# An expert layer whose tiles run two narrow experts, two wide, two narrow, two wide, instead of four wide and then four narrow

## The chip, the core and the metric

The kernel runs on one core of one Trainium2 chip. The metric is the device time of one execution in microseconds. A core has a matrix engine (TensorE, PE in the rows; its weight loads are PEld), a vector engine (VectorE, DVE), an engine for activations (ScalarE, ACT), GpSimd (POOL) and SyncE (SP), which here only issues transfers and passes on permissions. Each runs its own program, and they meet at semaphores.

## The reference, cut to what matters

A token embedding with a depthwise convolution over 31 positions, an attention layer that is linear in the sequence, and a mixture of experts, each added to the running `h`. 8 sequences of 512 tokens, 256 channels. The change concerns the expert layer:

```
EXPERT_SIZES = [(4, 256), (4, 512)]      # experts 0-3 narrow, 4-7 wide
probs = sigmoid(xf @ router_w.T)         # xf: 4096 tokens x 256
topw, sel = top_k(probs, 2)              # two experts a token
topw = topw / (topw.sum(-1) + 1e-20)
h = square(relu(xf @ W1e))               # 256 -> 256 or 512
y = h @ W2e                              # 256 or 512 -> 256
out = sum over the two chosen experts of weight * y
```

Float32 products are made of three products of parts (high by high, low by high, high by low).

## The kernel before, in words

**Up to 505 us** the kernel convolves, attends, and routes each batch. VectorE computes for each of a token's two choices a row in a queue in memory (`queue_d`), which has one stretch of rows for each expert, and GpSimd writes the token there with an indirect transfer. `expert_no` maps the eight positions of that order to experts: positions 0 to 3 are the wide experts, 4 to 7 the narrow ones. The weights in the core's memory (`w1_first`, `w1_second`, `w2_hi`, `w2_lo`) lie in the order of positions, each with room for 512 columns; GpSimd clears the half that a narrow expert leaves (lines 845 to 853 and 1576 to 1578).

**The table.** After the last batch VectorE turns the counts of the experts into a table, in a chain of tiny operations that each wait for the one before (`chained`, from line 1221): for each tile of 128 queue rows its first row, its expert (`word_of`, eight tiles in a register's value, three bits each) and `apart`, 16 where a tile has another expert than the tile before it and 0 elsewhere.

**The expert stage** takes 71 tiles of 128 rows, which is the most that any routing can need. For this input the counts of tokens that the reference's own router gives are 1122, 690, 757, 1416 for the narrow experts and 1410, 792, 824, 1181 for the wide ones, so in tiles 9, 6, 6, 12 and 12, 7, 7, 10: 69 tiles with tokens and two of filler. In the order before, tiles 0 to 35 are wide, 36 to 68 narrow, and expert changes lie at tiles 12, 19, 26, 36, 45, 51, 57 and 69 (the filler).

Step j of the pipeline does on TensorE `up(j)`, the turning of x for tile j+2, `act_turn(j-1)` and `down(j-2)`; on ScalarE `relu(j)`, `x_hi(j+2)`, `a_hi(j-1)` and `y(j-2)`; on VectorE `act_w(j)` and the low parts. Two steps make a turn; steps 2n and 2n+1 are turn n. `all_turns` (lines 1522 to 1538) asks once a turn, with a branch on each of the three engines, which width the turn has, and every fourth turn each loads the next word of the table (turns 0, 4, 8, ...). Before the change the width of a turn is that of its oldest tile, 2n-2: with the wide tiles first this is never too narrow. A turn is wide or narrow as a whole.

**The adds.** `y` has four places (`RING`). Tile j's y is added into the output by an indirect transfer from GpSimd (line 1583), and `y(j)` on ScalarE waits until the add of tile j-4, which had the same place, has landed. SyncE permits each add (`allow`, line 1553; its `sem_inc` on line 1563): it waits for `y_ready`, and then for the three adds before, in one of two ways. Tiles of one expert hold different tokens, so their adds may be in flight together. At a tile of another expert (`apart` is 16) all adds before it must have landed. And the first adds have constants for waits, where the value in the register cannot be zero:

```
if before < RING:
    sp.wait_ge(added[before % RING], 16)
else:
    wait_apart(sp, added[before % RING], differs16 + 16 * (before // RING), sp_passed)
```

so adds 1, 2, 3 and 4 each wait until the add ahead of them has landed, whatever their experts.

## Time and profile before

| | us |
|---|---|
| median of 3 runs (lowest to highest) | 737.45 (732.85 to 738.35) |
| the profiled execution | 736.28 |
| its span, first to last instruction | 734.6 |
| share of the span in which TensorE is busy | 86% |
| the chain that ended last: share of TensorE | 65% |
| the same: transfer of the adds (out<-y) | 5% |
| the expert stage, first product to the end | 509.79 to 734.6 |

The page gives each engine's busy time and its share of the span, the span in 40 slices, and the chain of work that ended last. In the slices TensorE stands at 9 tenths and more in the wide part of the expert stage, and at 8 in the narrow part. A busy TensorE is not one at its peak, since the ends of its products are modelled. The granted clock is given as a share of 2.4 GHz: 1.00 is that level and 0.50 is 1.2 GHz. Rows of a timeline begin with the start in us and the duration in us; a bracket gives the idle time ahead and what ended it.

### The profile page before, as it was taken

What the parts mean: (1) busy time and instruction counts of PE and PEld (TensorE: products, weight loads), DVE (VectorE), ACT (ScalarE), POOL (GpSimd) and SP (SyncE); (2) the same over time, 40 slices, a digit from 0 to 9 for tenths busy, and PEclk for the clock granted to TensorE, in tenths of its full rate; (3) what the DMA queues carried; (4) which work ended last, traced back from release to release, by engine and by line L of the source; (5) the groups of instructions that cost most, each with busy time, mean ns of one, the idle gap of its engine ahead of it and who ended that gap; (6) DMA issues with size and microseconds to landing.
All of it is one profiled execution on the core that took longest, in us unless ns stands there. A gap on an engine that the chain in (4) does not pass through costs nothing.

```text
span 734.6 us, 15772 instructions
## 1 busy us (share of the span) xinstructions
PE 632.1 (86%) x5032; PEld 547.8 (75%) x5032; DVE 469.7 (64%) x1216; ACT 306.8 (42%) x668; POOL 322.0 (44%) x292
## 2 busy tenths in 40 slices
PE   6997579999999999999999997523999999988881
PEld 6897457787877878778778785512899999987871
DVE  6475585777779777797787963573554554555540
ACT  3460135343353443533435335330544544555541
POOL 6350250330814608237073260635254454466574
PEclk9999689999999999999999999855999999999996
DMA  6551990010111101112010010423355445466663
GB/s 227 191 105 23 207 341 11 2 57 3 58 58 52 66 1 60 57 45 73 2 59 30 31 57 2 143 95 108 52 83 81 75 82 81 76 112 111 106 97 45
DMA packets 37216, 58.12 MB, mean 79 GB/s; under 512 B 5726, under 2 KB 31066, under 8 KB 36506
## 3 DMA queue, kind: packets, MB, share of 16 engines
q1 hardware_dynamic: 22434, 36.14, 16.9%
q0 software_dynamic: 14160, 20.13, 15.3%
q8 instruction: 61, 1.00, 0.6%
q10 hardware_dynamic: 520, 0.51, 0.2%
q14 instruction: 41, 0.34, 0.2%
HBM read 28.30 MB, written 27.42 MB: 76 GB/s over the span
## 4 chain that ended last, share of the span: by engine, by line
PE 65%; DVE 11%; DMA 7%; issue 5%; ACT 5%; POOL 3%; SPq 3%; DVEq 0%; POOLq 0%; ACTq 0%
PE bank L1311 20%; PE bank L1703 16%; PE bank L1383 8%; DMA out<-y,token_at 5%; PE bank L1354 4%; PE bank L1371 2%; PE bank L1719 2%; PE bank L521 2%; PE bank L522 2%; DVE xn L1009 2%; PE bank L542 2%; PE bank L1340 2%; POOL out L1583 2%; ACT k_exps L895 2%; DVE row L1089 1%
## 5 line engine op out<-in xcount | busy, mean ns | idle before, releaser
L1583 POOL DMA_INDIRECT out<-y,token_at x71 | 111.6, 1572 | 109.7 <-SPq L1563 107.6
L839 POOL DMA_INDIRECT queue_d<-row,slot x64 | 68.8, 1075 | 165.8 <-DVE slot L1148 148.7
L1660 DVE SCALAR_TENSOR_TENSOR act_w<-relu,queue_rows 128x512 f32<-128x512 f32 (+1 forms) x71 | 44.6, 629 | 102.5 <-ACT relu L1606 52.3
L1311 PE MATMUL bank<-xt_hi,w_first 128*128 128x512 f32 x256 | 95.1, 417 | 0.9 <-DVE second_half L1026 0.9
L1311 PE MATMUL bank<-w_first,xt_hi 128*128 128x512 f32 x256 | 83.8, 409 | 2.2 <-DVE xt_lo L1016 1.5
L831 POOL TENSOR_TENSOR second_half<-second_half,q_inv 128x512 f32<-128x512 f32 x64 | 64.9, 1041 | 44.0 <-DVE q_inv L1035 43.8
L887 ACT ACTIVATE second_half<-second_half 128x512 f32<-128x512 f32 x64 | 39.6, 632 | 87.9 <-DVE second_half L1026 87.9
L895 ACT ACTIVATE k_exps<-bank,k_negmax 128x512 f32<-128x512 f32 x64 | 44.1, 690 | 75.3 <-DVE k_negmax L1042 75.1
L1703 PE MATMUL bank<-w_hi,a_hi 128*128 x214 | 66.0, 308 | 1.6 <-DVE a_lo L1666 1.1
L1703 PE MATMUL bank<-w_lo,a_hi 128*128 x214 | 59.9, 280 | 0.1
L1606 ACT ACTIVATE relu<-bank 128x512 f32<-128x512 f32 (+1 forms) x71 | 35.4, 498 | 58.7 <-PE bank L1703 57.9
L1703 PE MATMUL bank<-w_hi,a_lo 128*128 x214 | 59.6, 278 | 0.0
L1311 PEld LDWEIGHTS bank<-w_first,xt_hi 128*128 128x128 f32 x256 | 46.9, 192 | 15.6 <-issue 2.7
L1383 PE MATMUL bank<-g,wv_t 128*128 128x256 f32 x256 | 56.7, 380 | 1.2 <-ACT g L877 1.2
L1311 PEld LDWEIGHTS bank<-xt_hi,w_first 128*128 128x128 f32 x256 | 49.2, 192 | 11.3 <-DVE second_half L1026 1.8
L1023 DVE TENSOR_REDUCE q_max<-bank 128x8 f32<-128x512 f32 x64 | 42.1, 657 | 22.6 <-PE bank L1311 22.6
L1383 PEld LDWEIGHTS bank<-g,wv_t 128*128 128x128 f32 x256 | 48.6, 190 | 8.4 <-ACT g L877 1.6
L1042 DVE TENSOR_REDUCE k_negmax<-bank 128x1 f32<-128x512 f32 x64 | 42.8, 680 | 13.4 <-PE bank L1311 13.1
L1311 PE MATMUL bank<-w_first,xt_lo 128*128 128x512 f32 x128 | 50.9, 398 | 0.0
L1311 PE MATMUL bank<-xt_lo,w_first 128*128 128x512 f32 x128 | 50.8, 397 | 0.0
L1703 PE MATMUL bank<-w_first,x_hi 128*128 x142 | 40.1, 364 | 9.7 <-DVE x_lo L1648 6.5
L1693 PE MATMUL bank<-ident,queue_rows 128*128 128x128 f32 x142 | 27.7, 279 | 23.3 <-DMA queue_rows<-queue_d 23.3
(183 smaller groups left out, 1564.3 us busy)
## 6 DMA issues: line engine op xcount, KB each, us to landing
queue_rows<-queue_d SPq DMA_DIRECT2D x71, 129.0 KB, 2.3
store<-in_L_ffn_w SPq DMA_DIRECT2D x4, 1536.0 KB, 9.2
out<-res SPq DMA_DIRECT2D x8, 512.0 KB, 2.9
h_d<-store SPq DMA_DIRECT2D x6, 512.0 KB, 9.0
h_in<-h_d SPq DMA_DIRECT2D x6, 512.0 KB, 4.0
windows<-taps_d SPq DMA_DIRECT2D x4, 512.0 KB, 5.8
wqk<-in_L_attn_w_qkv SPq DMA_DIRECT2D x1, 2048.0 KB, 13.9
out<-y,token_at POOLq DMA_INDIRECT x71, 4.0
```

The costliest lines, as they stand in the source:

```text
L831: nc.gpsimd.tensor_tensor(v, v, q_inv[:, b.par, u].unsqueeze(2).to_broadcast([P, 8, DH]), ALU.mult).then_inc(q_ready, 1)
L839: pool.indirect_dma_start(out=queue_d, in_=row[:, t, c, :], in_offset=None, out_offset=bass.IndirectOffsetOnAxis(ap=slot[:, TT * c + t:TT ...
L887: nc.scalar.activation(v, v, ACT.Exp, scale=SCALE).then_inc(q_exp_ready, 1)
L895: nc.scalar.activation(k_exps[:, c % 2], qk_bank(10 + c)[:], ACT.Exp, bias=k_negmax[:, c:c + 1], accum_out=k_sum[:, b.par, c:c + 1]).then_ ...
L1023: link(nc.vector.tensor_reduce(q_max[:, u % 2], src, AX, ALU.max), q_chain, b, Q_LINKS, 2 * u + 1 - (u > 0))
L1042: nc.vector.tensor_reduce(k_negmax[:, c:c + 1], qk_bank(10 + c)[:], AX, ALU.max, negate=True).then_inc(k_max_ready, 1)
L1311: last = nc.tensor.matmul(o, a, c, start=(n == 1), stop=(n == 3 * len(pairs)))
L1383: last = nc.tensor.matmul(tail_bank(6)[:, DIM * kk:DIM * kk + DIM], wv_t[:, a, P * kk:P * kk + P], g[:, a], start=(a == 0), stop=(a == PAI ...
L1583: pool.indirect_dma_start(out=out, in_=y[:, j % RING, :], in_offset=None, compute_op=ALU.add, out_offset=bass.IndirectOffsetOnAxis(ap=toke ...
L1606: nc.scalar.activation(relu[:, u % 2, 0:width], bank[2 + u % 2][:, 0:width], ACT.Relu).then_inc(relu_ready, 1)
L1660: nc.vector.scalar_tensor_tensor(out=act_w[:, u % 2, 0:width], in0=relu[:, u % 2, 0:width], scalar=rows[:, u, DIM:DIM + 1], in1=relu[:, u ...
L1703: last = nc.tensor.matmul(o, a, c, start=(n == 1), stop=(n == parts))
```

## The change

The order of positions becomes two narrow, two wide, two narrow, two wide: positions 0, 1, 4, 5 are experts 0 to 3 and positions 2, 3, 6, 7 experts 4 to 7. So a position is wide when its second bit is set. The pieces in which the weights are split and the halves that are cleared follow (lines 605 and following, `w1_pads`, the w2 pads). Filler tiles take position 0, a narrow one, where they took 7.

The width of a turn now comes from a new table, `kind_of`, of one bit for a turn: set when any of the four tiles 2n-2 to 2n+1 is wide. VectorE computes it at the end of the table's chain. All three engines load it every eighth turn; only TensorE still loads `word_of`. Since a narrow turn can now come ahead of a wide one, the upper halves of `act_w`, `a_hi` and `a_lo` are read before anything wrote them, and GpSimd clears them once, after the table is ready. ScalarE, VectorE and TensorE wait for that.

With the counts above, tiles 0 to 14 are narrow, 15 to 33 wide, 34 to 51 narrow, 52 to 68 wide and the two of filler narrow. Expert changes lie at tiles 9, 15, 27, 34, 40, 52, 59 and 69. Turns 0 to 6, 18 to 25 and 36 are narrow, and 7 to 17 and 26 to 35 wide: 21 wide turns, where turns 0 to 18 were wide, 19. Adds 1 to 4 wait as before.

```diff
--- before
+++ changed
@@ -79,6 +79,8 @@
 TABLE = -(-TILES // SLOTS) * SLOTS
 FILLERS = TABLE - TOKENS * TOPK // P
 TURN = 2
+TURNS = -(-(TILES + AHEAD) // TURN)
+TURN_WORDS = -(-TURNS // SLOTS)
 RING = 4
 TOTAL_W = sum(WIDTHS)
@@ -127,6 +129,7 @@
         self.tile_no = sbuf("tile_no", [1, TABLE])
         self.row_of = sbuf("row_of", [1, TABLE], I32)
         self.word_of = sbuf("word_of", [1, TABLE // SLOTS], I32)
+        self.kind_of = sbuf("kind_of", [1, TURN_WORDS], I32)
         self.apart = sbuf("apart", [1, TABLE], I32)
         self.consts, self.filler_ready, self.ends_ready, self.filled, self.chain, self.ready = (sem(n) for n in (
@@ -602,16 +605,16 @@
     r = store[:, n % 3]
     if n < KC:
         own = NARROW * NARROW_W
-        return [(r[:, 0:own].rearrange("p (e w) -> p e w", w=NARROW_W),
-                 dst[:, WIDE * MAXW:].rearrange("p (e w) -> p e w", w=MAXW)[:, :, 0:NARROW_W]),
-                (r[:, own:], dst[:, 0:WIDE * MAXW])]
+        dst = dst.rearrange("p (h e w) -> p h e w", h=2, w=MAXW)
+        return [(r[:, 0:own].rearrange("p (h e w) -> p h e w", h=2, w=NARROW_W), dst[:, :, 0:2, 0:NARROW_W]),
+                (r[:, own:].rearrange("p (h e w) -> p h e w", h=2, w=MAXW), dst[:, :, 2:4])]
     r = r.rearrange("p (c n) -> p c n", n=DIM)
     if n == KC:
-        return [(r[:, 0:8].rearrange("p (e c) n -> p e (c n)", c=2),
-                 dst[:, WIDE * FC:].rearrange("p (e c) n -> p e (c n)", c=FC)[:, :, 0:2 * DIM]),
-                (r[:, 8:12], dst[:, 0:4])]
-    return [(r, dst[:, 4:WIDE * FC])]
+        return [(r[:, 0:8].rearrange("p (h e c) n -> p h e (c n)", h=2, c=2),
+                 dst[:].rearrange("p (h e c) n -> p h e (c n)", h=2, c=FC)[:, :, 0:2, 0:2 * DIM]),
+                (r[:, 8:12], dst[:, 2 * FC:3 * FC])]
+    return [(r[:, 0:4], dst[:, 3 * FC:4 * FC]), (r[:, 4:12], dst[:, 6 * FC:8 * FC])]
 def attend(nc, ctx, sem, bank, ident, base, base0, rw_t, w1, w2, h_d, store, h_in, loaded, h_stored, raw_in,
@@ -767,10 +770,10 @@
         nc.gpsimd.memset(minus_half[:], -0.5).then_inc(consts_pool, 1)
         nc.gpsimd.memset(before[:], 1.0).then_inc(consts_pool, 1)
         nc.gpsimd.memset(every[:], 1.0).then_inc(consts_pool, 1)
-        nc.gpsimd.iota(expert_no[:, 0:WIDE], [[1, WIDE]], base=NARROW, channel_multiplier=0,
-                       allow_small_or_imprecise_dtypes=True).then_inc(consts_pool, 1)
-        nc.gpsimd.iota(expert_no[:, WIDE:], [[1, NARROW]], base=0, channel_multiplier=0,
-                       allow_small_or_imprecise_dtypes=True).then_inc(consts_pool, 1)
+        by_kind = expert_no[:].rearrange("p (h k e) -> p k h e", h=2, k=2)
+        for kind in range(2):
+            nc.gpsimd.iota(by_kind[:, kind], [[2, 2], [1, 2]], base=NARROW * kind, channel_multiplier=0,
+                           allow_small_or_imprecise_dtypes=True).then_inc(consts_pool, 1)
         nc.gpsimd.iota(base0[:], [[QROWS, EXPERTS]], base=0, channel_multiplier=0,
                        allow_small_or_imprecise_dtypes=True).then_inc(consts_pool, 1)
         nc.gpsimd.iota(base[:], [[QROWS, EXPERTS]], base=0, channel_multiplier=0,
@@ -848,9 +851,8 @@
             pool.wait_ge(tail_psum, last.nth(TAIL_USES, 2))
             for kk in range(KC):
                 for part in range(2):
-                    pad = w1_parts[kk][:, part].bitcast(F32)[:, WIDE * MAXW:]
-                    nc.gpsimd.memset(pad.rearrange("p (e w) -> p e w", w=MAXW)[:, :, NARROW_W:MAXW], 0.0
-                                     ).then_inc(w1_zero, 1)
+                    pad = w1_parts[kk][:, part].bitcast(F32).rearrange("p (h e w) -> p h e w", h=2, w=MAXW)
+                    nc.gpsimd.memset(pad[:, :, 0:2, NARROW_W:MAXW], 0.0).then_inc(w1_zero, 1)
         def step(b, prev, nxt, old):
             enqueue(old)
@@ -1211,9 +1213,9 @@
         space, at = x2_t[:].rearrange("p k n -> p (k n)"), [0]
-        def taken(rows, n):
+        def taken(rows, n, within=space):
             at[0] += n
-            return space[0:rows, at[0] - n:at[0]]
+            return within[0:rows, at[0] - n:at[0]]
         passed = taken(1, TABLE * EXPERTS).rearrange("p (t e) -> p t e", e=EXPERTS)
         upto_tiles = taken(P, EXPERTS * EXPERTS).rearrange("p (t e) -> p t e", e=EXPERTS)
@@ -1249,7 +1251,31 @@
         chained(nc.vector.memset(differs[:, 0:1], 0.0))
         chained(nc.vector.tensor_tensor(differs[:, 1:], expert_f[:, 1:], expert_f[:, 0:TABLE - 1], ALU.not_equal))
         chained(nc.vector.tensor_scalar(table.apart[:], differs, 16.0, None, ALU.mult))
-        chained(nc.vector.tensor_scalar(expert_f, expert_f, float(EXPERTS - 1), None, ALU.min))
+        chained(nc.vector.tensor_scalar(differs, expert_f, float(EXPERTS) - 0.5, -float(EXPERTS), ALU.is_gt, ALU.mult))
+        chained(nc.vector.tensor_tensor(expert_f, expert_f, differs, ALU.add))
+        done, at[0] = passed.rearrange("p t e -> p (t e)"), 0
+        wide_i, wide = taken(1, TABLE, done).bitcast(I32), taken(1, TABLE, done)
+        in_pair, in_turn = taken(1, TABLE // TURN, done), taken(1, TURN_WORDS * SLOTS, done)
+        turns2, turns4 = (taken(1, TURN_WORDS * SLOTS // m, done) for m in (2, 4))
+        chained(nc.vector.tensor_copy(wide_i, expert_f))
+        chained(nc.vector.tensor_scalar(wide_i, wide_i, 1, 1, ALU.logical_shift_right, ALU.bitwise_and))
+        chained(nc.vector.tensor_copy(wide, wide_i))
+        pairs = wide.rearrange("p (n u) -> p n u", u=TURN)
+        nc.vector.memset(in_turn, 0.0)
+        chained(nc.vector.tensor_tensor(in_pair, pairs[:, :, 0], pairs[:, :, 1], ALU.max))
+        chained(nc.vector.tensor_copy(in_turn[:, 1:TABLE // TURN + 1], in_pair))
+        chained(nc.vector.tensor_tensor(in_turn[:, 0:TABLE // TURN], in_turn[:, 0:TABLE // TURN], in_pair, ALU.max))
+        pairs = in_turn.rearrange("p (n u) -> p n u", u=2)
+        chained(nc.vector.scalar_tensor_tensor(out=turns2, in0=pairs[:, :, 1], scalar=2.0, in1=pairs[:, :, 0],
+                                               op0=ALU.mult, op1=ALU.add))
+        pairs = turns2.rearrange("p (n u) -> p n u", u=2)
+        chained(nc.vector.scalar_tensor_tensor(out=turns4, in0=pairs[:, :, 1], scalar=4.0, in1=pairs[:, :, 0],
+                                               op0=ALU.mult, op1=ALU.add))
+        pairs = turns4.rearrange("p (n u) -> p n u", u=2)
+        chained(nc.vector.scalar_tensor_tensor(out=table.kind_of[:], in0=pairs[:, :, 1], scalar=16.0,
+                                               in1=pairs[:, :, 0], op0=ALU.mult, op1=ALU.add))
         pairs = expert_f.rearrange("p (n u) -> p n u", u=2)
         chained(nc.vector.scalar_tensor_tensor(out=word2, in0=pairs[:, :, 1], scalar=float(EXPERTS),
@@ -1520,17 +1546,20 @@
         if value > 0:
             engine.wait_ge(s, value)
-    def all_turns(engine, step):
-        words = []
-        for first in range(0, TILES + AHEAD, TURN):
-            if first % SLOTS == 0 and first < TILES:
+    def all_turns(engine, step, by_expert=False):
+        words, kinds = [], []
+        for n in range(TURNS):
+            first = n * TURN
+            if n % SLOTS == 0:
+                kinds.append(engine.value_load(table.kind_of[0:1, n // SLOTS:n // SLOTS + 1], min_val=0,
+                                               max_val=2 ** SLOTS - 1))
+            if by_expert and first % SLOTS == 0 and first < TILES:
                 words.append(engine.value_load(table.word_of[0:1, first // SLOTS:first // SLOTS + 1], min_val=0,
                                                max_val=EXPERTS ** SLOTS - 1))
-            oldest = max(first - AHEAD, 0)
-            with engine.If(((words[oldest // SLOTS] >> (3 * (oldest % SLOTS))) & (EXPERTS - 1)) < WIDE):
+            with engine.If(((kinds[-1] >> (n % SLOTS)) & 1) > 0):
                 for j in range(first, first + TURN):
                     step(words, j // SLOTS, j % SLOTS, MAXW)
             with engine.Else():
@@ -1574,10 +1603,12 @@
     def gpsimd(pool):
         attention_left(pool)
         for w in (w2_hi, w2_lo):
-            pad = w[:].bitcast(F32)[:, WIDE * FC:].rearrange("p (e c) n -> p e (c n)", c=FC)
-            nc.gpsimd.memset(pad[:, :, 2 * DIM:], 0.0).then_inc(pads_zero, 1)
+            pad = w[:].bitcast(F32).rearrange("p (h e c) n -> p h e (c n)", h=2, c=FC)
+            nc.gpsimd.memset(pad[:, :, 0:2, 2 * DIM:], 0.0).then_inc(pads_zero, 1)
         pool.wait_ge(table.ready, 1)
+        for beyond in (act_w, a_hi, a_lo):
+            nc.gpsimd.memset(beyond[:].bitcast(F32)[:, :, NARROW_W:], 0.0).then_inc(pads_zero, 1)
         for j in range(TILES):
             pool.wait_ge(may_add, j + 1)
             pool.indirect_dma_start(
@@ -1634,6 +1665,7 @@
         x_high(0, 0)
         x_high(1, 1)
         act.wait_ge(table.ready, 1)
+        act.wait_ge(pads_zero, 5)
         all_turns(act, step)
     def vector(dve):
@@ -1682,6 +1714,7 @@
         x_low(0, 0)
         x_low(1, 1)
         dve.wait_ge(table.ready, 1)
+        dve.wait_ge(pads_zero, 5)
         all_turns(dve, step)
     def tensor(pe):
@@ -1745,7 +1778,7 @@
             if j == 2:
                 pe.wait_ge(w2_lo_ready, 2)
-                pe.wait_ge(pads_zero, 2)
+                pe.wait_ge(pads_zero, 5)
             if 2 <= j <= TILES + 1:
                 down(j - 2, u, expert_at(words, j - 2), width)
@@ -1754,7 +1787,7 @@
         pe.wait_ge(table.ready, 1)
         pe.wait_ge(w1_lo_ready, KC)
         pe.wait_ge(w1_zero, 2 * KC)
-        all_turns(pe, step)
+        all_turns(pe, step, by_expert=True)
     return Programs(sync, gpsimd, scalar, vector, tensor)
```

ScalarE where the expert stage begins (`w_hi` is the high part of the second weights, `x_hi` that of the first two tiles). Before:

```order
L1594 ACTIVATE w_hi<-store 128x1024
L1594 ACTIVATE w_hi<-store 128x3072 [waits raw_in3]
L1601 ACTIVATE x_hi<-bank 128x256 [waits x_turned] x2
L1530 TENSOR_LOAD word_of [waits table_ready]
L1530 ISA x2
L1533 REGISTER_ALU
L1533 COMPARE_AND_BRANCH
L1606 ACTIVATE relu<-bank 128x512 [waits up_done]
```

and with the change:

```order
L1625 ACTIVATE w_hi<-store 128x1024
L1625 ACTIVATE w_hi<-store 128x1024 [waits raw_in3]
L1625 ACTIVATE w_hi<-store 128x2048
L1632 ACTIVATE x_hi<-bank 128x256 [waits x_turned] x2
L1557 TENSOR_LOAD kind_of [waits pads_zero,table_ready]
L1557 ISA x2
L1562 REGISTER_ALU
L1562 COMPARE_AND_BRANCH
L1637 ACTIVATE relu<-bank 128x512 [waits up_done]
```

The last piece of the second weights is two operations instead of one, and the first relu stands behind a wait for GpSimd's clearing.

GpSimd in the same place, from the last writes to the queue on. Before:

```order
L839 DMA queue_d<-row,slot 34816x258 [waits slots_ready]
L839 DMA queue_d<-row,slot 34816x258 x7
L1578 MEMSET w_hi 128x4x512 [waits stored1,stored0]
L1578 MEMSET w_lo 128x4x512
L1583 DMA out<-y,token_at 4224x256 [waits may_add,table_ready]
```

and with the change:

```order
L842 DMA queue_d<-row,slot 34816x258 [waits slots_ready]
L842 DMA queue_d<-row,slot 34816x258 x7
L1607 MEMSET w_hi 128x2x2x512 [waits stored1,stored0]
L1607 MEMSET w_lo 128x2x2x512
L1611 MEMSET act_w 128x2x256 [waits table_ready]
L1611 MEMSET a_hi 128x2x256
L1611 MEMSET a_lo 128x2x256
L1614 DMA out<-y,token_at 4224x256 [waits may_add] x71
```

The three clearings of 512 numbers a partition stand behind the two that were there, and ahead of the adds.

## Rows read from the trace of the kernel before

**Rows 1.** Windows of 10 us, one wide and one narrow: busy times, clock, DMA

```profile
core 0: us, PE busy (x) PEld busy (x) DVE busy (x) ACT busy (x) POOL busy (x), PEclk, DMA share, GB/s
600.00:610.00 10.00, 10.00 (x73) 9.17 (x72) 5.23 (x12) 5.25 (x12) 4.66 (x3) 1.00 0.48 76
660.00:670.00 10.00, 8.84 (x76) 8.46 (x74) 5.45 (x18) 5.83 (x18) 5.36 (x5) 1.00 0.60 99
```

**Rows 2.** Waits from 640 to 735 us: total us, times, longest us

```profile
ACT y L1618 <- DMA out<-y,token_at: 14.4, 12, 2.8
```

**Rows 3.** Timeline of ScalarE: y of tiles 0, 35, 49 and 68

```profile
519.55 0.38 ACT L1618 ACTIVATE y<-bank 128x256 f32<-128x256 f32 x1 [0.89 <-PE bank L1703]
...
640.00 0.38 ACT L1618 ACTIVATE y<-bank 128x256 f32<-128x256 f32 x1 [0.66 <-PE bank L1703]
...
672.94 0.39 ACT L1618 ACTIVATE y<-bank 128x256 f32<-128x256 f32 x1 [2.17 <-DMA out<-y,token_at]
...
717.15 0.39 ACT L1618 ACTIVATE y<-bank 128x256 f32<-128x256 f32 x1 [0.27 <-PE bank L1703]
```

**Rows 4.** Timeline of ScalarE: relu of the first step of turns 22, 23, 24

```profile
654.57 0.38 ACT L1606 ACTIVATE relu<-bank 128x256 f32<-128x256 f32 x1 [0.96 <-PE bank L1703]
...
658.97 0.39 ACT L1606 ACTIVATE relu<-bank 128x256 f32<-128x256 f32 x1 [1.02 <-PE bank L1703]
...
663.83 0.38 ACT L1606 ACTIVATE relu<-bank 128x256 f32<-128x256 f32 x1 [1.51 <-PE bank L1703]
```

**Rows 5.** Timeline of GpSimd: adds 0, 3, 4, 35, 43, 44, 45, 68

```profile
520.75 1.61 POOL L1583 DMA_INDIRECT out<-y,token_at  x1 [13.84 <-SPq L1563]
...
533.48 1.56 POOL L1583 DMA_INDIRECT out<-y,token_at  x1 [2.77 <-SPq L1563]
539.32 1.70 POOL L1583 DMA_INDIRECT out<-y,token_at  x1 [4.27 <-SPq L1563]
...
641.74 1.55 POOL L1583 DMA_INDIRECT out<-y,token_at  x1 [1.88 <-SPq L1563]
...
660.92 1.55 POOL L1583 DMA_INDIRECT out<-y,token_at  x1 [0.44 <-SPq L1563]
662.94 1.56 POOL L1583 DMA_INDIRECT out<-y,token_at  x1 [0.47 <-SPq L1563]
667.72 1.55 POOL L1583 DMA_INDIRECT out<-y,token_at  x1 [3.22 <-SPq L1563]
...
720.73 1.56 POOL L1583 DMA_INDIRECT out<-y,token_at  x1 [0.30 <-issue]
```

**Rows 6.** The tile `y`: its transfers, min/median/max us

```profile
DMA to landing us min/median/max: 3.8/4.0/5.1
```

**Rows 7.** The tile `queue_rows`: `act_w` by width

```profile
L1660 DVE SCALAR_TENSOR_TENSOR act_w<-relu,queue_rows x71: 467/750/784, 513.4 to 716.6; 128x512 f32<-128x512 f32 x38, 128x256 f32<-128x256 f32 x33
```

**Rows 8.** Chain of waits, in order of time: `up` of tiles 0 and 2

```profile
509.79 2.92 PE bank L1703 x6
...
515.86 1.40 PE bank L1703 x6
```

**Rows 9.** Timeline: table's end, last clearing, first row loads, first relu

```profile
494.43 0.16 DVE L1261 SCALAR_TENSOR_TENSOR word_of<-x_t 1x9 int32<-1x9 f32 x1
...
505.08 1.82 POOL L1578 MEMSET w_lo<- 128x2048 f32 x1
505.84 3.48 SPq L1551 DMA_DIRECT2D queue_rows<-queue_d  x7
...
512.75 0.60 ACT L1606 ACTIVATE relu<-bank 128x512 f32<-128x512 f32 x1 [3.18 <-PE bank L1703]
```

**Rows 10.** Windows of 2 us, columns as in rows 1

```profile
104.00:106.00 2.00, 0.41 (x2) 0.41 (x3) 2.00 (x6) 0.78 (x2) 1.50 (x2) 0.72 0.95 271
458.00:460.00 2.00, 0.85 (x4) 0.78 (x5) 0.00 (x0) 1.99 (x4) 1.55 (x2) 1.00 0.20 68
508.00:510.00 2.00, 1.36 (x5) 0.79 (x6) 0.82 (x2) 0.77 (x2) 0.00 (x0) 0.50 0.90 254
```

## The prediction

> **What bounds the kernel now.** I began with the windows of the expert stage, since everything that the change touches lies there. In a wide window TensorE is busy all the time and every other engine about half of it, at the full clock; in a narrow one TensorE is at 8.84 of 10 us and GpSimd has more to do than before [rows 1]. So the wide part is TensorE's, and the narrow part is close to a balance between TensorE and the adds. The waits say the same: from 640 us on ScalarE waits 12 times for an add to land before it may write y [rows 2]. Then I read the pace of each. From y(0) at 519.55 to y(35) at 640.00 are 35 wide steps, 3.44 us each [rows 3]. A narrow turn takes 4.40 us, 2.20 a step, and 4.86 with a load of the table, 0.46 more [rows 4]. SyncE lets adds of one expert go 2.02 us apart when they stand in line (660.92 to 662.94), which is only just faster than 2.20; I take 2.08, since others lie a little wider. At a change of expert the gap was 4.78 (662.94 to 667.72), and before add 69 it cannot be shorter than a landing, 3.8 to 5.1 us [rows 5, 6]; I take 4.45. From an add to the y that has its place again it was 5.22 at the longest (667.72 to 672.94) [rows 3, 5] and cannot be under 3.8 [rows 6]; I take 4.7. An add without a line ahead starts 1.74 after its y (640.00 to 641.74) [rows 3, 5].
>
> **The adds at the start are the row that matters most.** Adds 1 to 4 are serial by their constants. Add 0 starts at 520.75, add 3 at 533.48, three gaps of 4.24 us, and add 4 at 539.32, 5.84 later: 18.57 us for four gaps [rows 5]. With wide steps this is free: y(8) needs add 4, 539.32 + 4.7 = 544.0, and comes by itself at 519.55 + 8 x 3.44 = 547.1. With narrow steps it is not.
>
> **The sum, tile by tile.** 38 steps were wide, which is turns 0 to 18 [rows 7]; 42 will be.
>
> 1. Start to y(0). At the low clock `up(0)` takes 2.92 us, at the higher `up(2)` takes 1.40 [rows 8]. Half the columns save 1.4 in the first, about 1.0 in the second, 0.7 in the third, and half the products of `down(0)` 0.7: 3.8 in all. But the low level then covers more of the steps; I give back 1.3. So y(0) comes 2.5 us earlier (1.0 to 3.8), at 517.0.
> 2. Add 0 starts 1.2 later as before (520.75 - 519.55) [rows 3, 5], at 518.2; add 4 at 518.2 + 18.6 = 536.8; y(8) at 541.5. TensorE alone would be there after four turns and one table load, 517.0 + 17.6 + 0.5 = 535.1. The stall is 6.4, of which TensorE, half a microsecond ahead, keeps 0.5 back: 5.9 us lost. With four gaps of 4.24 and a return of 4.2 it is 3.8; with the return of 5.2 it is 6.4.
> 3. Tile 9 has a new expert. Add 8 cannot start before 536.8 + 4 x 2.08 = 545.1, add 9 at 549.6, so y(13) at 554.3. TensorE needs half a turn, a narrow turn and wide turn 7 from y(8): 2.2 + 4.4 + 6.9 - 0.5 = 13.0, 554.5. Nothing more is lost. y(13) at 554.4.
> 4. y(33) is 20 wide steps on: 623.2.
> 5. y(49) is eight narrow turns and two table loads on: 36.1, 659.3. The change at tile 34 puts add 34 at 623.2 + 1.74 + 4.45 = 629.4, add 39 at 639.8, add 40 (a change again) at 644.2, y(44) at 648.9; TensorE alone: 623.2 + 24.2 + 0.5 = 647.9. A loss of 1.0 less 0.5: 659.8.
> 6. y(67) is 18 wide steps on: 721.7, and y(68) 3.4 later, 725.1.
> 7. Add 68 follows 1.74 later, as it does behind wide tiles, at 726.9. What follows (add 69 behind the change to the filler, add 70, the landing) is what followed before: 734.6 - 720.73 = 13.87 [rows 5]. End at 740.7.
>
> **The same by differences.** Six more of the steps behind y(0) are wide (41 for 35): 6 x 1.24 = +7.5. Start -2.5. Stall at the start +5.9, in the second stretch +0.5, one table load fewer -0.5. Before, y(68) came at 717.15, where 640.00 + 33 x 2.20 + 4 x 0.46 gives 714.4: 2.7 us of waits for adds, which go. And add 68 stood 3.58 behind its y for 1.74 in an empty line: -1.8 [rows 3, 5]. Sum +6.4, against 740.7 - 734.6 = +6.1 above. The two agree within their rounding; I take 6.1. So the line of adds is emptied as the wide tiles in the middle and at the end promise, worth 4.5 us, and it is paid with more wide steps and with the serial adds.
>
> **What I cost at nothing.** VectorE's table grows by 11 operations of about 0.2 us, to 496.9 from 494.6 us; the row loads behind it start at 505.84, held by the last writes to the queue [rows 9]. If that cover were gone it would be 2.3. GpSimd's three clearings have a quarter of the size of the one that took 1.82: about 0.5 each, 506.9 to 508.4 [rows 9]. ScalarE and VectorE wait for them ahead of the first relu and `act_w`, and every later step of theirs is queued behind; but the first relu was at 512.75 and comes near 511.3 now. If the 2.9 us of cover were gone, each further one would count in full. GpSimd's adds, queued behind the clearings, begin 10 us later. TensorE's second table load at turn 0 lies ahead of `up(0)`: 0 to 0.46. The further operation for the second weights falls where ScalarE is idle.
>
> **A rule against the row.** The adds land in 3.8 to 5.1 us, 4.0 in the middle, and the serial gaps are 4.24 and more [rows 5, 6]. The Trainium skill (DMA: Bandwidth & Descriptors, Anatomy of one DMA) puts the fixed cost of a transfer at about 2.0 us and the rest at bytes over 436 GB/s; by that an estimate for a gap is some 2.6 us, the stall of step 2 is gone and the sum is 5.9 lower. The trace does not agree, so the sum goes by the rows.
>
> **Rivals.**
>
> *The serial adds do not bind* (10%). Here the first adds would be quicker than before, since only narrow work is about. It decides below 3.05 us a gap: y(8) at 535.1 needs add 4 at 530.4, four gaps in 12.2. Against it: no landing is under 3.8 [rows 6]. For it: the fourth gap, 5.84 where the three before are 4.24, looks disturbed, so part of the 18.57 may go. The span would be 734.8: no slower than now, 737.7 on the median's scale.
>
> *The clock falls in the gaps of the start* (14%). For tiles 4 to 8 TensorE works some 1.8 us in each 4.2. For it: at 104 us, with 0.41 us of work in 2, the granted clock went to 0.72, and at 508 it stood at 0.50, which is 1.2 GHz [rows 10]. Against it: at 458 us, with 0.85 in 2, it stayed at 1.00 [rows 10]. In the gaps themselves a fall costs nothing, but the steps to y(13) would run at half speed for about as long as the start needed, 5 us from 509.8: half of that is lost, +2.5, so 746.1. The Trainium skill (TensorE: Matmul & The Clock Gate, HAM oscillation) tells of kernels in which waits for transfers throttle TensorE again and again; by that rule this case would be the likely one, and the rows at 458 us speak against it.
>
> *The second narrow stretch loses as the one before did* (12%). It holds 16 narrow steps; the 33 before lost 2.7 and ended with a line. If each change of expert costs 5.2 and each return 5.2, both at the long end of their rows, y(44) comes at 650.9 for 648.9: 745.6.
>
> *The start is late* (6%): GpSimd or the table holds the first steps by 2 us or more, 745.6 and up.
>
> *The width bits are wrong or too wide* (2%): a turn that need not be wide costs 2.5 us, all sixteen narrow ones 40.
>
> **Numbers.** The span is forecast at 740.7 and the profiled execution at 740.7 + 1.7 = 742.4 (it was 736.28 for a span of 734.6). The median of the runs stood 1.2 above the profiled one, so the time is 743.6, rounded to **744**, 0.9% more than 737.45. This forecast has 50%. Its own range is 740 to 747, from the bounds of steps 1 and 2. A measurement of this kernel can tell about 1% from no change; the border, 744.8, runs through the forecast, so I give it 30% within and 20% slower. The rivals add 10 + 2 + 4 + 2 points within 1%, and 12 + 8 + 4 + 2 slower. The rest, 6%, is for what I have not seen: 4 faster, 2 within. Together faster 4%, same 50%, slower 46%. The range is 737 to 749: it takes in the first rival and the clock, and leaves out a start that is much too late and anything faster than now.
>
> **What would show it.** Step 1: y(0) near 517. Step 2: five adds 4.1 us or more apart from about 518, ScalarE's y(5) to y(8) waiting for the transfer of the adds, y(8) near 541.5; if y(8) is near 535 the first rival holds. Step 4: 3.44 us a step in both wide stretches. Step 5: y(33) to y(49) in 36 to 37 us. Step 7: add 68 within 2 us of y(68), and 13.9 us to the end. `act_w` should be 42 times 512 wide, less the one of step 71 that does not exist. The clock row at 525 to 545 decides the second rival. I am wrong at the root if waits of ScalarE for adds are short in the first 25 us of the stage, or if wide steps take other than 3.44.

## The result, and the profile after

The changed kernel takes 745.34 us (median of 4 runs, 742.21 to 748.63), the kernel before in the same comparison 735.15 (4 runs, 732.22 to 738.35). The ratio is 1.0127, 95% interval 1.0069 to 1.0184: slower by 9.3 us, with 5.1 to 13.5 inside the interval. Forecast were 744 us and an increase of 6.1. In a second comparison, with 5 runs of the changed kernel and 12 of the kernel before, the ratio was 1.0135 (1.0111 to 1.0158), at 754.89 us for 745.79. One run of the kernel before in a later comparison, at 945.67 us and a granted clock of 0.65, is a slow one and stands in no ratio here.

The profiled execution took 748.63 us, its span is 746.9. It is 12.3 us longer than the span of before, and not all of that belongs to the expert stage. The first row load comes at 509.91 us instead of 505.84 [rows 9], and most of the difference is there already when the attention begins. So I compare the stage alone, from the first row load to the last instruction: 734.6 - 505.84 = 228.8 us before, 746.9 - 509.91 = 237.0 after, +8.2.

`act_w` by width, from the tile `queue_rows` of the kernel after, answers to [rows 7]:

```profile
L1692 DVE SCALAR_TENSOR_TENSOR act_w<-relu,queue_rows x71: 483/751/800, 517.0 to 730.1; 128x512 f32<-128x512 f32 x41, 128x256 f32<-128x256 f32 x30
```

41 wide where 38 were: the change does what it says. The timeline of ScalarE after, with y of tiles 0, 6, 7, 8, 13, 14, 33, 49 and 68, answers to [rows 3]. Start and duration in us, in brackets the idle time ahead and what ended it:

```profile
521.50 0.38 ACT L1649 ACTIVATE y<-bank 128x256 f32<-128x256 f32 x1 [0.21 <-PE bank L1736]
...
535.63 0.39 ACT L1649 ACTIVATE y<-bank 128x256 f32<-128x256 f32 x1 [0.58 <-DMA out<-y,token_at]
539.84 0.39 ACT L1649 ACTIVATE y<-bank 128x256 f32<-128x256 f32 x1 [2.72 <-DMA out<-y,token_at]
544.60 0.38 ACT L1649 ACTIVATE y<-bank 128x256 f32<-128x256 f32 x1 [3.45 <-DMA out<-y,token_at]
...
558.07 0.38 ACT L1649 ACTIVATE y<-bank 128x256 f32<-128x256 f32 x1 [0.70 <-PE bank L1736]
562.20 0.38 ACT L1649 ACTIVATE y<-bank 128x256 f32<-128x256 f32 x1 [0.67 <-PE bank L1736]
...
628.20 0.39 ACT L1649 ACTIVATE y<-bank 128x256 f32<-128x256 f32 x1 [0.67 <-PE bank L1736]
...
665.24 0.39 ACT L1649 ACTIVATE y<-bank 128x256 f32<-128x256 f32 x1 [0.25 <-PE bank L1736]
...
731.33 0.38 ACT L1649 ACTIVATE y<-bank 128x256 f32<-128x256 f32 x1 [0.73 <-PE bank L1736]
```

y(6), y(7) and y(8) each wait for an add to land, and y(8) comes 23.1 us after y(0), where eight narrow steps alone take 18.2 (measured below). From y(13) to y(14) it is 4.13 us, where a wide step takes 3.44. Adds 0 to 4 and 68 on GpSimd after answer to [rows 5]:

```profile
522.19 1.61 POOL L1614 DMA_INDIRECT out<-y,token_at  x1 [13.19 <-SPq L1592]
527.20 1.73 POOL L1614 DMA_INDIRECT out<-y,token_at  x1 [3.40 <-SPq L1592]
531.66 1.56 POOL L1614 DMA_INDIRECT out<-y,token_at  x1 [2.73 <-SPq L1592]
535.93 1.56 POOL L1614 DMA_INDIRECT out<-y,token_at  x1 [2.71 <-SPq L1592]
540.12 1.56 POOL L1614 DMA_INDIRECT out<-y,token_at  x1 [2.63 <-SPq L1592]
...
733.12 1.56 POOL L1614 DMA_INDIRECT out<-y,token_at  x1 [1.94 <-SPq L1592]
```

Four serial gaps take 17.93 us. Add 68 follows its y by 1.79 us, where it stood 3.58 behind before: the line of adds at the end is gone, as promised.

| us | before | forecast | after |
|---|---|---|---|
| first row load to y(0) | 13.71 | 11.2 | 11.59 |
| y(0) to y(8) | 27.56 | 24.5 | 23.10 |
| y(8) to y(13) | 17.19 | 12.9 | 13.47 |
| y(13) to y(33) | 68.85 | 68.8 | 70.13 |
| y(33) to y(49) | 39.79 | 36.6 | 37.04 |
| y(49) to y(68) | 44.21 | 65.3 | 66.09 |
| y(68) to add 68 | 3.58 | 1.7 | 1.79 |
| add 68 to the end | 13.87 | 13.9 | 13.78 |
| stage | 228.8 | 234.9 | 237.0 |

### The profile page after: what moved, and what is told of

The parts are those of the page before. It is cut to its first block, busy times and chain, and to the rows that moved or that the text cites. A ratio compares the mean times of both kernels' runs of the same rounds, so it can differ in the third digit from the quotient of the medians.

```text
span 746.9 us, 15984 instructions
## 1 busy us (share of the span) xinstructions
PE 643.9 (86%) x5078; PEld 558.9 (75%) x5078; DVE 473.3 (63%) x1228; ACT 309.7 (41%) x669; POOL 320.4 (43%) x295
## 4 chain that ended last, share of the span: by engine, by line
PE 67%; DVE 12%; DMA 8%; ACT 5%; issue 5%; SPq 2%; POOL 2%; DVEq 0%; POOLq 0%; ACTq 0%
PE bank L1337 20%; PE bank L1736 17%; PE bank L1409 8%; DMA out<-y,token_at 5%; PE bank L1380 4%; PE bank L1752 3%; PE bank L1397 2%; PE bank L524 2%; PE bank L525 2%; DVE xn L1011 2%; PE bank L545 2%; PE bank L1366 2%; ACT k_exps L897 2%; PE bank L1726 2%; DVE k_negmax L1044 1%
## 5 line engine op out<-in xcount | busy, mean ns | idle before, releaser
L842 POOL DMA_INDIRECT queue_d<-row,slot x64 | 65.5, 1023 | 165.7 <-DVE slot L1150 148.7
L1736 PE MATMUL bank<-w_hi,a_hi 128*128 x226 | 69.6, 308 | 0.6 <-ACT y L1649 0.4
L1736 PE MATMUL bank<-w_lo,a_hi 128*128 x226 | 63.3, 280 | 0.0
L1736 PE MATMUL bank<-w_hi,a_lo 128*128 x226 | 63.1, 279 | 0.0
L1409 PE MATMUL bank<-g,wv_t 128*128 128x256 f32 x256 | 58.3, 387 | 1.2 <-ACT g L879 1.2
```

The source lines that it names most:

```text
L842: pool.indirect_dma_start(out=queue_d, in_=row[:, t, c, :], in_offset=None, out_offset=bass.IndirectOffsetOnAxis(ap=slot[:, TT * c + t:TT ...
L1409: last = nc.tensor.matmul(tail_bank(6)[:, DIM * kk:DIM * kk + DIM], wv_t[:, a, P * kk:P * kk + P], g[:, a], start=(a == 0), stop=(a == PAI ...
L1736: last = nc.tensor.matmul(o, a, c, start=(n == 1), stop=(n == parts))
```

## The experiments

Two theories stood, and the expectations below name them. **Theory A**: the order costs, by the serial adds under narrow steps and by more wide steps. **Theory B**: the added machinery costs (bits, clears, a second table), whatever the order. Ratios below are to the kernel before, on the same chip; "before, words early" and "all cures" ran on a chip on which it took 735 us, the others where it took 746 to 747. The stage is that of one execution, the profiled one, while a ratio is over all runs of its comparison; where the two disagree, the ratio is the safer of them.

| kernel | ratio, 95% interval | stage, us |
|---|---|---|
| changed, again | 1.0135 (1.0111 to 1.0158) | 237.1 |
| adds not serial | 1.0069 (1.0049 to 1.0088) | 234.1 |
| bits loaded early | 1.0087 (1.0068 to 1.0106) | 233.7 |
| old order with the bits | 1.0050 (1.0027 to 1.0073) | 232.8 |
| before, adds not serial | 1.0004 (0.9989 to 1.0019) | 229.1 |
| wide first | 1.0044 (1.0030 to 1.0059) | 232.7 |
| both cures | 1.0013 (0.9998 to 1.0029) | 229.1 |
| wide ends, bits early | 1.0019 (1.0002 to 1.0035) | 231.8 |
| before, words early | 1.0025 (0.9996 to 1.0054) | 229.3 |
| all cures | 1.0000 (0.9975 to 1.0025) | 227.3 |
| rows ahead | 1.0124 (1.0095 to 1.0152) | 236.0 |
| all cures, rows ahead | 0.9969 (0.9954 to 0.9985) | 227.7 |

**The changed kernel again.** No edit.

> The changed kernel once more, beside the kernel before on the same chip. If the loss is in the expert stage (theory A), the stage from the first row load to the end is again 8 us longer than the 228.8 us of before, whatever happens ahead of it. If part of the loss lies ahead of the stage and belongs to the change (theory B), the first row load is again about 4 us later than 505.8; if that part was luck of the clock (theory A again), it comes anywhere between 505 and 510. Ratio to the kernel before 1.010 to 1.015 either way.

The stage is 237.1 us, the first row load at 514.40. That says nothing of the change: a kernel with the old order had it at 516.5 on this chip, and another at 518.4 on a second chip that is as slow. The kernel before takes 735 us on one chip and 746 to 747 on three others, and most of that lies ahead of the stage; between executions it is several us more. So the stages are what I compare, beside the ratios.

**Adds not serial.**

```diff
-            if j >= RING:
+            if j >= 1:
                 differs16 = sp.value_load(table.apart[0:1, j:j + 1], min_val=0, max_val=16)
+            early = [before for before in range(max(0, j - RING + 1), j) if before < RING]
+            if early:
+                with sp.If(differs16 > 0):
+                    for before in early:
+                        sp.wait_ge(added[before % RING], 16)
             for before in range(max(0, j - RING + 1), j):
-                if before < RING:
-                    sp.wait_ge(added[before % RING], 16)
-                else:
+                if before >= RING:
                     wait_apart(sp, added[before % RING], differs16 + 16 * (before // RING), sp_passed)
```

> The changed kernel, but adds 1 to 6 wait for the adds before them only where the tile has another expert (a branch on SyncE), which never happens in the first nine tiles. Theory A (the serial adds stall the narrow start): y(8) comes about 18 us after y(0) instead of 23.1, no wait of ScalarE for an add in the first 25 us, the stage 5 us shorter, about 232, ratio to the kernel before about 1.006. Theory B (the loss is in the added tables, clears and wide turns): stage unchanged at 237.

The timeline of ScalarE in this kernel, y of tiles 0, 7 and 8:

```profile
529.24 0.38 ACT L1652 ACTIVATE y<-bank 128x256 f32<-128x256 f32 x1 [0.24 <-PE bank L1739]
...
545.01 0.38 ACT L1652 ACTIVATE y<-bank 128x256 f32<-128x256 f32 x1 [0.20 <-PE bank L1739]
547.39 0.38 ACT L1652 ACTIVATE y<-bank 128x256 f32<-128x256 f32 x1 [0.20 <-PE bank L1739]
```

No wait for an add is left here, and y(0) to y(8) takes 18.15 us, 5.0 less than 23.1. The ratio falls by 0.0066, 4.9 us. The stage of the profiled execution fell by only 3.0: from y(33) to y(49) it took 38.85, 1.6 more than in the changed kernel beside it. Most of that is one step, y(45) to y(46), with 4.41 for 3.26. Windows of 2 us over it, columns as in [rows 1]:

```profile
658.00:660.00 2.00, 1.05 (x8) 0.77 (x6) 1.21 (x4) 1.27 (x5) 1.56 (x1) 1.00 0.80 137
660.00:662.00 2.00, 1.37 (x6) 1.38 (x7) 0.00 (x0) 0.32 (x1) 1.55 (x1) 0.67 0.81 123
662.00:664.00 2.00, 2.00 (x12) 2.00 (x11) 1.28 (x4) 1.16 (x3) 1.56 (x1) 0.50 0.80 128
664.00:666.00 2.00, 2.00 (x19) 2.00 (x19) 0.54 (x3) 1.32 (x4) 1.55 (x1) 0.97 0.82 139
```

TensorE waits 1.6 us for a low part from VectorE, and then its granted clock is 0.50 for about 3.4 us. At 1.00 the same work takes half of that, so by an estimate from these rows the fall costs up to 1.7 us, and this stage would be near 232.5 without it. That fits the ratio and the expectation, both at about 5 us. Three of the profiles below have such a fall in their narrow tiles too: "before, adds not serial", "wide ends, bits early" and "before, words early". Each of their stages may hold up to 1.7 us of it; those of the kernel before and of the changed kernel hold none there.

**Bits loaded early.**

```diff
+    def load_kinds(engine):
+        return [engine.value_load(table.kind_of[0:1, n:n + 1], min_val=0, max_val=2 ** SLOTS - 1)
+                for n in range(TURN_WORDS)]
...
-            if n % SLOTS == 0:
-                kinds.append(engine.value_load(table.kind_of[0:1, n // SLOTS:n // SLOTS + 1], min_val=0,
-                                               max_val=2 ** SLOTS - 1))
...
+        act.wait_ge(table.ready, 1)
+        kinds = load_kinds(act)
         x_high(0, 0)
         x_high(1, 1)
```

and likewise on VectorE and TensorE, ahead of their first work on rows.

> The changed kernel, but each of the three engines loads all five words of the width bits ahead of its first work of the stage, where it waits for rows anyway, and none later. Theory A with the term that the forecast had not: the steps at turns 8, 16 and 32 fall from 4.1 us to 3.45, the one at turn 24 by 0.6, so the stage is 2 to 2.6 us shorter, 234.5. If these long steps come from something else in those turns (fetching of code), they stay and nothing changes.

The timeline of ScalarE in this kernel, y of tiles 13 and 14, beside 558.07 and 562.20 above:

```profile
561.95 0.39 ACT L1650 ACTIVATE y<-bank 128x256 f32<-128x256 f32 x1 [0.67 <-DMA out<-y,token_at]
565.38 0.39 ACT L1650 ACTIVATE y<-bank 128x256 f32<-128x256 f32 x1 [0.67 <-PE bank L1739]
```

The step of turn 8 falls from 4.13 to 3.43, and those of turns 16 and 32 from 4.05 and 4.22 to 3.42 and 3.43: 2.1 us. From the first row load to y(0) it is 10.28 instead of 11.78: 1.5 more, which I had not counted on. The stage is 3.4 us shorter and the ratio 0.0048 lower, 3.6 us. So it was the loads, not the fetching of code.

**Old order with the bits.** The pieces, `expert_no` and the clears as before the change, and the bit inverted:

```diff
-        chained(nc.vector.tensor_scalar(wide_i, wide_i, 1, 1, ALU.logical_shift_right, ALU.bitwise_and))
+        chained(nc.vector.tensor_scalar(wide_i, wide_i, 2, 1, ALU.logical_shift_right, ALU.bitwise_and))
         chained(nc.vector.tensor_copy(wide, wide_i))
+        chained(nc.vector.tensor_scalar(wide, wide, -1.0, 1.0, ALU.mult, ALU.add))
```

> The old order, four wide experts and then four narrow, with all the new machinery: the table of width bits, the three clears and the waits for them, loads of both tables. Theory A (the order costs, the machinery little): stage 228.8 to 231, which is 0.7 each for double loads in wide turns 8 and 16, ratio 1.000 to 1.003. Theory B (the machinery costs): stage near 237, ratio about 1.012.

The first row load and y(0), then y of tiles 13 and 14, in its timeline:

```profile
516.47 0.37 SPq L1581 DMA_DIRECT2D queue_rows<-queue_d  x1
...
531.46 0.38 ACT L1650 ACTIVATE y<-bank 128x256 f32<-128x256 f32 x1 [1.02 <-PE bank L1737]
...
576.38 0.38 ACT L1650 ACTIVATE y<-bank 128x256 f32<-128x256 f32 x1 [0.67 <-PE bank L1737]
580.42 0.39 ACT L1650 ACTIVATE y<-bank 128x256 f32<-128x256 f32 x1 [0.67 <-PE bank L1737]
```

The machinery costs 4.1 us in the stage and 3.7 by the ratio, more than my 0 to 2.2: 15.0 to y(0) for 13.7, 0.6 at each of turns 8 and 16, and the rest in the narrow half. Theory B has part of the loss: half of it by the stage (4.1 of 8.2 us), over a third by the ratio (0.0050 of 0.0135).

**Before, adds not serial.** The same edit of `allow`, in the kernel before.

> The control for the serial adds: the kernel before, with the same branch in place of the constant waits of adds 1 to 6. Theory A (a serial add of 4.3 us or more costs only where a step is shorter than that over the ring, so not with wide steps of 3.44): stage 228.8 as before, ratio 0.999 to 1.001, though adds 0 to 4 take 14 us instead of 18. If the serial adds cost something by themselves (their transfers at the start), it gains up to 2 us.

Its adds 0 and 4:

```profile
533.90 1.61 POOL L1586 DMA_INDIRECT out<-y,token_at  x1 [14.44 <-SPq L1566]
...
548.04 1.56 POOL L1586 DMA_INDIRECT out<-y,token_at  x1 [1.85 <-SPq L1566]
```

14.1 us for 18.6, and nothing is gained: ratio 1.0004 over 12 runs, and y(0) to y(8) in 27.57 us for 27.56. A serial add costs nothing under wide steps. It takes the narrow start for it to cost 5 us.

**Wide first**: two wide, two narrow, two wide, two narrow.

```diff
-                 dst[:].rearrange("p (h e c) n -> p h e (c n)", h=2, c=FC)[:, :, 0:2, 0:2 * DIM]),
-                (r[:, 8:12], dst[:, 2 * FC:3 * FC])]
+                 dst[:].rearrange("p (h e c) n -> p h e (c n)", h=2, c=FC)[:, :, 2:4, 0:2 * DIM]),
+                (r[:, 8:12], dst[:, 0:FC])]
...
-            nc.gpsimd.iota(by_kind[:, kind], [[2, 2], [1, 2]], base=NARROW * kind, channel_multiplier=0,
+            nc.gpsimd.iota(by_kind[:, kind], [[2, 2], [1, 2]], base=NARROW * (1 - kind), channel_multiplier=0,
```

> The order mirrored: two wide, two narrow, two wide, two narrow, all else as in the changed kernel (21 wide turns too). Theory A: the serial adds are covered, the line of adds at the end is back. y(0) to y(8) in 27.6 us, no stall; the stage 234 us, 3 less than the changed kernel's 237, ratio to the kernel before 1.007. If the stall at the start were not what the order costs, the stage would stay at 237.

y(0) to y(8) in 27.69 us, and the stage is 232.7, 4.4 less than that of the changed kernel; the ratio is 0.0091 lower, 6.8 us. So the mirrored order, with as many wide turns and as many loads, costs half as much by the stage (3.9 us for 8.3) and a third by the ratio. The line of adds at the end, which I had expected back, did not come: add 68 starts 1.55 behind y(68).

**Both cures** in the changed kernel.

> The changed kernel with both cures: adds 1 to 6 not serial, width bits loaded early. If the two losses are separate, they add: 3 and 3.4 us measured alone, so the stage is 230.5 and the ratio to the kernel before 1.002. If the second cure only moved work into the stall of the first, the sum is smaller than its parts: 232 to 233.

229.1 us and 1.0013. Together the cures bring 8.0 us of stage, nearly all of the 8.2, and 0.0122 of ratio, where they brought 0.0066 and 0.0048 alone. So the two losses are separate. The stages alone gave less, 3.0 and 3.4, since the first of them holds the fall of the clock.

**Wide ends, bits early**: two wide, four narrow, two wide.

```diff
-        chained(nc.vector.tensor_copy(wide_i, expert_f))
-        chained(nc.vector.tensor_scalar(wide_i, wide_i, 1, 1, ALU.logical_shift_right, ALU.bitwise_and))
+        chained(nc.vector.tensor_scalar(wide_i, expert_f, 2.0, None, ALU.add))
+        chained(nc.vector.tensor_scalar(wide_i, wide_i, 2, 1, ALU.logical_shift_right, ALU.bitwise_and))
         chained(nc.vector.tensor_copy(wide, wide_i))
+        chained(nc.vector.tensor_scalar(wide, wide, -1.0, 1.0, ALU.mult, ALU.add))
```

> Two wide, four narrow, two wide, width bits loaded early. Wide tiles cover the serial adds at the start and empty the line of adds at the end; there are still 21 wide turns. Theory A: y(0) to y(8) in 27.6 us, add 68 within 2 us of y(68), stage 231, ratio 1.003. For this order to beat the kernel before, the two emptied lines would have to be worth more than the two further wide turns; I expect they are not.

231.8 us and 1.0019, which is 1.4 us. Add 68 is 1.8 us behind y(68). Neither the stall nor the line is there, and it still does not beat the kernel before. That two more wide turns eat what the adds give back is my reading of this; no run has the one without the other. The stage is a poor witness here: this execution took 752.18 us, where the median of the twelve is 748.07, and from 633 to 636 us, in the narrow tiles, the granted clock is 0.50.

**Before, words early.** In the kernel before, all nine words of the table are loaded ahead of the first rows, as above with the bits.

> The kernel before, but every engine loads all nine words of the table ahead of its first work of the stage and none later. The third term of the loss seen from the other side: in the narrow half of the kernel before, turns 20, 24, 28 and 32 are 0.5 us longer for a load. If those loads set the pace there, the stage is up to 2 us shorter than 228.8 and the ratio 0.997 to 0.999. If the line of adds sets it, the steps get shorter at those turns and the waits for adds take it back: ratio 1.000.

Waits of ScalarE for adds in the stage, total us, times, longest: first in the kernel before, then in this one.

```profile
ACT y L1618 <- DMA out<-y,token_at: 14.4, 12, 2.8
```

```profile
ACT y L1618 <- DMA out<-y,token_at: 26.3, 22, 3.8
```

The loads at the narrow turns are gone, and y waits 11.9 us more for adds. The stage is 229.3 and the ratio 1.0025 (0.9996 to 1.0054), so nothing is gained: the second half of the expectation. In the kernel before, the narrow half is set by the adds as much as by TensorE. One caution: in this profile the granted clock is 0.50 from 707 to 710 us, which may hide a gain of up to 1.7 us in this stage; the ratio is over 12 runs and does not rest on this one.

**All cures**: the changed order, adds not serial, both tables loaded early.

> The changed order with adds 1 to 6 not serial and both tables loaded ahead of the stage. Against the version with the two cures (229.1 us) the loads at turns 4, 20 and 24 go, 0.6 each: stage 227.5, ratio to the kernel before 0.998 to 1.001, so at best level with it. If more than that is gained, the loads cost more than their own steps show.

227.3 us, ratio 1.0000 (0.9975 to 1.0025). By the stages the freed loads are a gain with wide tiles between the narrow ones, 229.1 to 227.3: 0.8 in y(0) to y(8) and 0.8 in y(33) to y(49), where loads stood. The ratios, 1.0013 and 1.0000 on two chips, do not tell the two kernels apart. By the ratio it is level with the kernel before.

**Rows ahead.** Theory A puts the stall at the start down to the adds alone. But in the timeline of TensorE after, a wait of 3.2 us is ended by a row load, whose issue stands in that of SyncE:

```profile
544.03 0.69 PE L1726 MATMUL bank<-ident,queue_rows 128*128 128x128 f32 x2 [3.22 <-DMA queue_rows<-queue_d]
```

```profile
540.62 0.34 SPq L1580 DMA_DIRECT2D queue_rows<-queue_d  x1
```

These are the rows of tile 13, loaded only at 540.62, since SyncE issues them in program order behind the permit for add 4; y(8) waited for that add until 544.60. (The expectation below has both one too low: tile 12 and add 3.) Two lines are late at the same moment, and the experiments so far do not say which one sets the pace. Here the rows are asked for one tile earlier, ahead of that permit:

```diff
+        load(SLOTS, row_at(SLOTS))
...
-            if j + SLOTS < TILES:
-                load(j + SLOTS, row_at(j + SLOTS))
+            if j + SLOTS + 1 < TILES:
+                load(j + SLOTS + 1, row_at(j + SLOTS + 1))
```

> The changed kernel, but SyncE issues each row load one tile earlier, ahead of the permit for the add before. In the profile of the changed kernel TensorE stands still from 540.8 to 544.0 for the rows of tile 12, which SyncE issued only at 540.62, since the load stood behind the serial permit of add 3. Two lines were late at the same moment: the add that y(8) waits for, and this load. If the adds alone set the pace (theory A as forecast), the stillness of TensorE and the fall of its clock go or get shorter, and y(0) to y(13) stays at 36.5 us, the stage at 237, ratio 1.0127 to 1.0135. If the serial adds cost by holding back the row loads, y(0) to y(8) falls by 1 to 3 us and the stage with it, to 234 to 236.

y of tiles 7 and 8 in its timeline, and windows over what follows, columns as in [rows 1]:

```profile
545.08 0.38 ACT L1650 ACTIVATE y<-bank 128x256 f32<-128x256 f32 x1 [3.05 <-DMA out<-y,token_at]
...
549.48 0.39 ACT L1650 ACTIVATE y<-bank 128x256 f32<-128x256 f32 x1 [3.09 <-DMA out<-y,token_at]
```

```profile
544.00:546.00 2.00, 1.46 (x13) 1.22 (x12) 0.13 (x1) 0.92 (x3) 0.62 (x1) 1.00 0.25 42
546.00:548.00 2.00, 1.01 (x7) 0.78 (x7) 1.08 (x4) 0.39 (x2) 1.23 (x2) 1.00 0.41 81
548.00:550.00 2.00, 1.58 (x12) 1.15 (x10) 0.00 (x0) 0.52 (x2) 1.33 (x2) 1.00 0.66 119
550.00:552.00 2.00, 0.72 (x4) 0.49 (x5) 1.21 (x4) 1.04 (x4) 1.48 (x1) 1.00 0.61 107
```

TensorE has work in every window and keeps 1.00. y(0) to y(13) takes 36.33 us, for 36.57 and 37.98 in the two profiles of the changed kernel. Those two have a long step, the one with two table loads, in different places; by y(14) it is 40.09 for 40.70 and 40.86. So the late rows made the stillness, and they and the fall of the clock together cost 0.6 to 0.8 us. The rest of the stall is the adds: with rows at hand, y(7) and y(8) still wait 3 us each for one. The stage is 1.0 shorter; the ratio, from four runs, is no different and could not show so little.

**All cures, rows ahead.** Both edits together.

> All cures (changed order, adds 1 to 6 not serial, both tables loaded early) and the row loads one tile earlier. With all cures no row load is waited for longer than 0.3 us, so this should change nothing: stage 227.3, ratio 0.999 to 1.001. It is the last candidate for a version ahead of the kernel before; a gain would show that the row loads still hold something that the waits don't show.

The ratio is 0.9969 (0.9954 to 0.9985), 2.3 us ahead of the kernel before, and the only one of these kernels ahead of it. That is a little better than I had expected. The stage of the profiled execution, 227.7, is no shorter than that of "all cures", 227.3, and 1.0 shorter than that of before. The interval of "all cures" reaches down to 0.9975. So no run shows that the rows ahead made the difference.

## Why the prediction was right, and where it was not

**The sign and the size** held: 744 for 745.34, with the forecast's own range at 740 to 747. But part of the nearness is luck: the kernel before came out at 735.15 in this comparison for the 737.45 on which the forecast stood, and 735.15 + 6.1 is 741.3. On its own scale the forecast was +6.1; the stage shows +8.2 and the ratio 9.3.

**Step 1, the start.** 2.12 us earlier for 2.5. The three clears took 0.54 each and ended at 509.0, ahead of the first row load, so costing them at nothing was right. What I had too low is the loads of the second table: I gave TensorE's 0 to 0.46, and taking it away brought 1.5 us, together with those on the other engines.

**Step 2, the serial adds.** The mechanism was right, the price 5.9 against 5.0 measured. The gaps took 17.93 us where I carried over 18.57, and an add was back after 4.48 (540.12 to 544.60) where I took 4.7. I named the adds behind SyncE's waits, not the row loads, which stand in the same queue: they came late too, and with the fall of the clock that followed it cost 0.6 to 0.8 us (40.09 us to y(14) without it, 40.70 and 40.86 with it).

**Step 3** lost nothing more to the adds at tile 9: 13.47 us, and 13.53 in the kernel without serial adds.

**Steps 4 and 6, the wide stretches: the term that was mis-sized.** I carried no price for a table load in a wide turn, because the kernel before shows next to none: its words are loaded at every fourth turn, and the step there takes 3.43 to 3.52 us. In the changed kernel TensorE loads from two tables at turns 8, 16 and 32, and these steps take 4.13, 4.05 and 4.22. That is 2.1 us, as much as the whole distance between forecast and measurement; the other misses (+0.4 at the start, -0.8 up to y(13), +0.4 in the second narrow stretch) cancel, which is luck. Without the second load the steps are back at 3.42 to 3.43. That one load is hidden behind the products that stand in line and two are not is my reading of it: no run has the new loads on one engine alone.

**Step 5** held, 37.04 for 36.6. **Step 7** held, 1.79 and 13.78 for 1.74 and 13.87.

**The sum of the loss.** The cures give 5.0 us for the serial adds (y(0) to y(8)) and 3.4 for the loads; what is left of 8.2 is near zero. So the difference between six more wide steps, +7.5, and the lines of adds that go, -4.5, with the earlier start, -2.5, is about nothing, as the differences in the forecast had it (+0.5). Only the sum of these three is shown by the kernel with both cures, not each of them.

**The rivals.** *The serial adds do not bind* is out: y(8) at 23.1. *The clock falls in the gaps* did happen. Windows of 2 us of the kernel after, columns as in [rows 1]:

```profile
540.00:542.00 2.00, 0.81 (x6) 0.61 (x6) 1.21 (x4) 1.15 (x4) 1.56 (x1) 1.00 0.18 33
542.00:544.00 2.00, 0.00 (x0) 0.00 (x0) 0.00 (x0) 0.00 (x0) 1.55 (x1) 1.00 0.76 114
544.00:546.00 2.00, 1.97 (x9) 1.98 (x10) 0.71 (x3) 1.21 (x4) 1.44 (x2) 0.50 0.78 132
546.00:548.00 2.00, 2.00 (x13) 2.00 (x13) 0.50 (x2) 0.71 (x3) 1.55 (x2) 0.65 0.82 129
```

TensorE does nothing from 542 to 544, waiting for the rows of tile 13, and then works at 0.50, 1.2 GHz, for about 3.4 us. The same fall stands in two other profiles with serial adds under narrow steps (the changed kernel again, and bits loaded early). With the rows ahead it is gone, with the adds as serial. I had priced it at 2.5 us; y(8) to y(13) took 13.47, 0.6 over the forecast, and 13.53 in the kernel without serial adds, which has no fall in these tiles. So the price was small, with the late rows 0.6 to 0.8 us: the line of adds held these tiles anyway. The row at 458 us, on which I called it unlikely, was a poor guide. It has 0.85 us of work in 2 at a clock of 1.00, and so have the windows with the rows ahead (0.72 to 1.58). But in the kernel with adds not serial the clock fell behind a window with 1.05 and a wait of 1.6 us, and in the three other profiles named there behind shorter waits still. So falls are not bound to the serial adds or to a window without work; what decides them these runs do not show. By the Trainium skill (TensorE: Matmul & The Clock Gate, HAM oscillation), waits for transfers throttle TensorE; the trace agrees that it falls behind a wait for rows, and the price was under 1 us here. *The second stretch loses as the one before did*: y(33) to y(49) lost 0.4 more than forecast, not 2. *The start is late*: by 0.4.

**What stays open.** The ratio gives 9.3 us, the stage 8.2; the interval allows for that, and no run shows a loss of the change ahead of the stage. How often the clock falls in the narrow tiles, in runs that were not profiled, is not known, so neither is its share in the ratios. What puts the last kernel 0.3% ahead, by 1.0 us of stage and the rest outside it, is open too. Why the two loads early in the stage cost 1.5 us together is not taken apart between the engines.

## What to carry to other kernels

When steps are put in another order, look for waits that are constants of the position and not of the work: here the first five adds were serial for a reason of the code, free under long steps, and 5 us under short ones. Price each new table load beside those that fall in the same turn, since a row that shows one load at next to no cost says nothing of two. Work that evens out two limits only pays if little is added at its borders: six more wide steps came with them here, by the forecast's rows 7.5 us for the 4.5 that the emptied line of adds gave back, and the evened-out order, with everything cured, came out 0.3% ahead of the plain one at best. And when two waits end within a microsecond, take one away to see which sets the pace: the one that left TensorE idle for 3.2 us here was worth under 1 us. And look at the clock in every profile whose stage disagrees with its ratio: one fall was worth up to 1.7 us here, as much as some of the effects that were sought.

## What the runs showed of the hardware

A table load on TensorE beside another in the same turn lengthened a wide step from 3.43 to between 4.05 and 4.22 us in the changed kernel, while one alone left it at 3.43 to 3.52 in the kernel before.

The granted clock fell to 0.50, which is 1.2 GHz, in seven of the fourteen profiles within the expert stage while TensorE still had work, each time for about 3.4 us. In three of them it followed a wait of 2.6 to 3.2 us for rows, under serial adds. In the other four it came in narrow tiles: after a wait of 1.6 us in one, and in three after waits under 0.7 us, with 0.95 to 1.43 us of work in the window of 2 us in which it began and in the one before. The kernel before and the one with both cures have waits of 1.1 us in narrow tiles and kept 1.00 there.

The lead-in, up to the first row load, lay between 505 and 519 us over these kernels, from chip to chip and run to run, which is more than any of the effects measured here. The stage repeated within 0.1 us in the one pair that there is (237.0 and 237.1), though its parts differed by up to 1.4 (y(0) to y(13) in 36.57 and 37.98).
